# Three of a tile step's four GpSimd powers taken in one instruction over twelve columns

## What is computed

```python
h  = layernorm(x) * (1 + ca) + sa                  # first normalization: mean and variance
# attention part
hn = w1 * (h * rsqrt(mean(h * h) + 1e-6))          # first RMS norm ("RMS1")
r, k, v, g, w = projections of hn mixed with the token before
S  = exp(-exp(w)) * S + k v                         # a scan over 1024 tokens, 16 heads of 8 x 8
o  = groupnorm(r (S + u k v)) * silu(g)
x1 = h + o @ Wo
h2 = w2 * (x1 * rsqrt(mean(x1 * x1) + 1e-6))       # second RMS norm ("RMS2")
y  = x1 + gelu(h2 @ ffn_w1) @ ffn_w2
x2 = x + ga * y
h3 = layernorm(x2) * (1 + cb) + sb                 # second layernorm ("LN2")
# expert part: softmax gate over 8 experts, the best two per token, gated units, weighted sum
out = x2 + gb * experts(h3)
```

## Time and profile before

| what | value |
|---|---|
| runs of the kernel | 724.88, 728.73 and 729.90 us; median 728.73 us |
| the profiled execution | 725.47 us, of which the profile's span is 723.8 us |
| busy share of the span | PE 85%, PEld 65%, DVE 83%, ACT 72%, POOL 74% |
| token stage | up to about 464 us of the span |
| expert stage | from there to 723.8 us |

### The profile page before, as it was taken

The page is one execution under the profiler, slowest core; times in us unless marked ns, Lnnn a source line. Parts: engine busy times, 40 slices in busy tenths (PEclk is TensorE's granted clock), DMA queues, the critical chain, the costliest instruction groups (busy, mean ns, idle before and its releaser), DMA issues. The chain is left out here.

```text
span 723.8 us, 14261 instructions
## 1 busy us (share of the span) xinstructions
PE 617.0 (85%) x3515; PEld 469.7 (65%) x3515; DVE 602.9 (83%) x1384; ACT 523.0 (72%) x1321; POOL 537.9 (74%) x657
## 2 busy tenths in 40 slices
PE   2556889999999999979789687737899999999994
PEld 0433566667777666648557565615688888888883
DVE  6389989999999999997999846665688888888884
ACT  2656668898888977976766676734677888788883
POOL 5467667899999779899869876575766666666666
PEclk8699989999999999998999899857999999999998
DMA  3999888889999898788778799525565444444420
GB/s 109 259 139 133 117 110 133 132 142 160 149 136 159 128 152 112 155 167 157 152 135 147 170 283 286 220 98 166 118 103 87 79 77 78 79 80 80 76 18 1
DMA packets 103300, 95.58 MB, mean 132 GB/s; under 512 B 14523, under 2 KB 82710, under 8 KB 102966
## 3 DMA queue, kind: packets, MB, share of 16 engines
q1 hardware_dynamic: 85846, 79.69, 58.3%
q0 software_dynamic: 16176, 12.75, 10.0%
q10 hardware_dynamic: 1200, 2.23, 0.9%
HBM read 35.47 MB, written 25.61 MB: 84 GB/s over the span
## 5 line engine op out<-in xcount | busy, mean ns | idle before, releaser
L2063 POOL DMA_INDIRECT out<-res,index x91 | 141.3, 1553 | 66.0 <-DVE res L2145 48.1
L843 POOL TENSOR_TENSOR rs_prod<-rT,state_rows 128x512 f32<-128x512 f32 x128 | 139.4, 1097 | 44.7 <-DVE state_rows L1528 43.2
L1281 PEld LDWEIGHTS ps_k<-w,gel 128*128 128x128 f32 x512 | 63.5, 205 | 16.8 <-issue 14.4
L1281 PE MATMUL ps_k<-w,gel 128*128 128x128 f32 x512 | 66.2, 291 | 2.4 <-ACT gel L1098 1.7
L2112 DVE SCALAR_TENSOR_TENSOR half<-ps_b,xg,sig 128x256 f32<-128x256 f32 x91 | 43.6, 480 | 26.0 <-ACT sig L1991 22.8
L1987 ACT ACTIVATE sig<-ps_a 128x256 f32<-128x256 f32 x91 | 35.1, 385 | 41.6 <-issue 20.7
L1246 PE MATMUL ps_f<-hnT_hi,mix_hi 128*128 128x512 f32 x128 | 54.7, 428 | 8.7 <-DVE hnT_lo L1651 7.6
L2105 DVE SCALAR_TENSOR_TENSOR ps_a<-ps_a,xg,sig 128x256 f32<-128x256 f32 x91 | 44.4, 488 | 10.8 <-ACT sig L1987 6.5
L1941 PEld LDWEIGHTS ps_y<-out_w,gT 128*128 128x128 f32 x364 | 47.3, 191 | 8.9 <-ACT gT L2020 5.2
L2013 ACT ACTIVATE ps_b<-bias_rows 128x512 f32 x89 | 53.0, 595 | 0.0
L1247 PE MATMUL ps_f<-hnT_lo,mix_hi 128*128 128x512 f32 x128 | 52.0, 406 | 0.0
(11 more groups left out here) (357 smaller groups left out, 1995.7 us busy)
## 6 DMA issues: line engine op xcount, KB each, us to landing
v_spread<-vT SPq DMA_DIRECT2D x128, 256.0 KB
xg<-sorted_scratch SPq DMA_DIRECT2D x91, 130.0 KB
xin<-in_L_attn_x SPq DMA_DIRECT2D x16, 256.0 KB, 6.3
x<-in_L_attn_x SPq DMA_DIRECT2D x16, 256.0 KB
out<-x SPq DMA_DIRECT2D x16, 256.0 KB
sorted_scratch<-gel SPq DMA_DIRECT2D x4, 910.0 KB, 8.0
tokens_scratch<-h SPq DMA_DIRECT2D x12, 256.0 KB
raw_w<-in_L_ffn_W ACTq DMA_DIRECT2D x2, 1024.0 KB, 8.1
```

Source lines behind the costliest of these rows:

```text
L843: pool.tensor_tensor(rs_prod[:, p, idx % 4], rT[p][:], state[idx][:, p * NT:(p + 1) * NT], ALU.mult).then_inc(s["rs_ready"], 1)
L1281: mm = pe.matmul(ps_k2[:, q * P:(q + 1) * P], gel[c][:, q * P:(q + 1) * P], w2[:, c, :], start=(c == 0), stop=(c == NF - 1))
L2063: pool.indirect_dma_start(out_rows, bass.IndirectOffsetOnAxis(ap=index[k % RESULTS][:, i:i + 1], axis=0), res[k % RESULTS][:, i, :], None, ...
```

## The change

The three roots of RMS1, RMS2 and LN2 are no longer taken one by one. `ve2`, `ve3`, `ve4` become slices of one tile `ve_all` of 12 columns, `rs2`, `rs3`, `rs4` slices of `rs_all`, and `minus_half` has 12 columns. POOL first does the additions of eps of all lanes that the step has, and then one `pow` over the columns of all of them. One semaphore, `roots_ready`, is raised once a step and takes the place of `rms1_rstd`, `rms2_rstd` and `ln2_rstd`; its count for tile `t` is `t` plus the lane's lag. Steps 7 to 16 have all three lanes (12 columns), steps 5, 6 and 17 to 20 have two (8 columns), the others one. LN1's root stays as it is.

```diff
-        minus_half = sb("minus_half", [P, NQ])
+        minus_half = sb("minus_half", [P, 3 * NQ])
...
+        ssq1, ve_all, rs_all = sb("ssq1", [P, NQ]), sb("ve_all", [P, 3 * NQ]), sb("rs_all", [P, 3 * NQ])
+        (ve2, ve3, ve4), (rs2, rs3, rs4) = ([each[:, i * NQ:(i + 1) * NQ] for i in range(3)] for each in (ve_all, rs_all))
+        RMS1, RMS2, LN2 = 1, 5, 7
...
+            def roots(lanes):
+
+                if lanes:
+                    for lane, t, done in lanes:
+                        after(pool, done, t)
+                    span = slice(lanes[0][0] * NQ, (lanes[-1][0] + 1) * NQ)
+                    pool.tensor_tensor(rs_all[:, span], ve_all[:, span], minus_half[:, span], ALU.pow).then_inc(s["roots_ready"], 1)
...
                 for t, p, b in tile(5):
                     after(pool, s["ssq3_ready"], t)
                     pool.tensor_scalar(ve3[:], ssq3[:], 1.0 / D, EPS_RMS, ALU.mult, ALU.add).then_inc(s["rms2_ve"], 1)
-                    after(pool, s["rms2_ve"], t)
-                    pool.tensor_tensor(rs3[:], ve3[:], minus_half[:], ALU.pow).then_inc(s["rms2_rstd"], 1)
                 for t, p, b in tile(1):
                     after(pool, s["ssq1_ready"], t)
                     pool.tensor_scalar(ve2[:], ssq1[:], 1.0 / D, EPS_RMS, ALU.mult, ALU.add).then_inc(s["rms1_ve"], 1)
-                    after(pool, s["rms1_ve"], t)
-                    pool.tensor_tensor(rs2[:], ve2[:], minus_half[:], ALU.pow).then_inc(s["rms1_rstd"], 1)
                 for t, p, b in tile(7):
                     after(pool, s["ln2_mv"], t)
                     after(pool, s["xn4_ready"], t - 1)
                     pool.tensor_scalar(shift4[:], mv4[:, :, 0], -1.0, 0.0, ALU.mult, ALU.add)
                     pool.tensor_scalar(ve4[:], mv4[:, :, 1], 1.0, EPS_LN, ALU.mult, ALU.add).then_inc(s["ln2_ve"], 1)
-                    after(pool, s["ln2_ve"], t)
-                    pool.tensor_tensor(rs4[:], ve4[:], minus_half[:], ALU.pow).then_inc(s["ln2_rstd"], 1)
-                    after(pool, s["ln2_rstd"], t)
+                roots([(lane, t, done) for lane, lag, done in ((0, RMS1, s["rms1_ve"]), (1, RMS2, s["rms2_ve"]), (2, LN2, s["ln2_ve"])) for t, p, b in tile(lag)])
+                for t, p, b in tile(7):
+                    after(pool, s["roots_ready"], t + LN2, 1, 0)
                     mean_shift(shift4, rs4, s["shift2_ready"])
...
             def normalize_second(t, p):
-                after(act, s["ln2_rstd"], t)
+                after(act, s["roots_ready"], t + LN2, 1, 0)
...
                 for t, p, b in tile(4):
-                    after(act, s["rms2_rstd"], t)
+                    after(act, s["roots_ready"], t + RMS2, 1, 0)
                     scale_rows(h2, h_all[:, t], rs3, s["h2_ready"])
...
                 for t, p, b in tile(0):
-                    after(act, s["rms1_rstd"], t)
+                    after(act, s["roots_ready"], t + RMS1, 1, 0)
                     scale_rows(hn, h_all[:, t], rs2, s["hn_ready"])
```

More of the change, by code:

```diff
@@ L443, in attention_block @@
         staged = h_all[:, TILES - 2:].rearrange("p n q d -> p (n q) d")[:, 0:6]
-        ssq1, ve2, rs2 = sb("ssq1", [P, NQ]), sb("ve2", [P, NQ]), sb("rs2", [P, NQ])
+        ssq1, ve_all, rs_all = sb("ssq1", [P, NQ]), sb("ve_all", [P, 3 * NQ]), sb("rs_all", [P, 3 * NQ])
+        (ve2, ve3, ve4), (rs2, rs3, rs4) = ([each[:, i * NQ:(i + 1) * NQ] for i in range(3)] for each in (ve_all, rs_all))
+        RMS1, RMS2, LN2 = 1, 5, 7
         hn = sb("hn", [P, NQ, P])
@@ L458, in attention_block @@
         o_sum = o_gated = sb("o_row", [P, NT])
-        ssq3, ve3, rs3 = sb("ssq3", [P, NQ]), sb("ve3", [P, NQ]), sb("rs3", [P, NQ])
+        ssq3 = sb("ssq3", [P, NQ])
         h2 = sb("h2", [P, NQ, P])
@@ L467, in attention_block @@
         st4, mv4, shift4 = sb("st4", [P, NQ, 6]), sb("mv4", [P, NQ, 2]), sb("shift4", [P, NQ])
-        ve4, rs4 = sb("ve4", [P, NQ]), sb("rs4", [P, NQ])
         h3 = [sb(f"h3{i}", [P, NQ, P]) for i in range(2)]
@@ L485, in attention_block @@
             "mod_ps mod_copied mod_step mod_ready mod_stored first_mods_ps first_mods_ready setup_step weights_step mix_ready "
-            "ln1_stats ln1_mv ln1_ve ln1_rstd xn1_ready h_scaled h_ready ssq1_ready rms1_ve rms1_rstd hn_ready "
+            "ln1_stats ln1_mv ln1_ve ln1_rstd xn1_ready h_scaled h_ready ssq1_ready rms1_ve roots_ready hn_ready "
             "hnT_ps hnT_ready hnlo_ready k_ps v_ps vT_ready "
@@ L490, in attention_block @@
             "o_ready osq_ready var_ps log_ready root_ready rootsq_ready weighed root_better rsg_ps onorm_ready ogated_ready wo_ps x1_ready "
-            "ssq3_ready rms2_ve rms2_rstd h2_ready h2T_ps h2T_ready h2lo_ready ffn2_ps y_ready y_gated x2_ready "
-            "shift1_ready shift2_ready scan_ready rs_ready kv_ready ln2_stats ln2_mv ln2_ve ln2_rstd xn4_ready h3_scaled h3_ready h3T_ps h3T_ready logits_ps logits_ready "
+            "ssq3_ready rms2_ve h2_ready h2T_ps h2T_ready h2lo_ready ffn2_ps y_ready y_gated x2_ready "
+            "shift1_ready shift2_ready scan_ready rs_ready kv_ready ln2_stats ln2_mv ln2_ve xn4_ready h3_scaled h3_ready h3T_ps h3T_ready logits_ps logits_ready "
             "small_ps small_ready expert_in expert_ps expert_hi expert_lo b1_ready b1_stored bias_in route_step tag_step rows_gated batch_staged tags_kept gain_ready exps_ready ranks_ps totals_ps totals_ready unlisted_ready blank_stored bias_rows_in last_staged gates_in gates_spread tags_set out_w_in listed table_step table_ps").split(),
@@ L974, in step @@
                     after(pool, s["ln1_ve"], t)
-                    pool.tensor_tensor(rs1[:], ve1[:], minus_half[:], ALU.pow).then_inc(s["ln1_rstd"], 1)
+                    pool.tensor_tensor(rs1[:], ve1[:], minus_half[:, 0:NQ], ALU.pow).then_inc(s["ln1_rstd"], 1)
                     after(pool, s["ln1_rstd"], t)
```

## The result

| what | before | changed kernel |
|---|---|---|
| median of six runs, taken together | 729.38 us (724.88 to 732.65) | 737.71 us (735.67 to 741.09) |
| ratio, with its 95% interval | 1 | 1.013 (1.010 to 1.016) |
| the profiled execution: span | 723.8 us | 737.7 us |
| end of the token stage in it | 477.40 us | 488.33 us |

The changed kernel is slower: the medians are 8.3 us, or 1.1%, apart, and the ratio is 1.013. The end of the token stage is taken here as the start of the expert stage's first DVE instruction. (The table ahead of the prediction gives about 464 us; that is where the last tiles' work thins out.)

A forecast was written before the change was run, and what follows sets the result against it. DVE was taken to set the pace without a gap in steps 7 to 11. 7.6 + 0.7 + 0.2 + 1.0 - 0.2 + 0.5 + 1.1 = 10.9 us on 725.5 or 728.7 us; 738.0 us said, range 728 to 745.

The forecast's parts named there:

- The chain: From DVE's moments over POOL's pow and ACT's square back to DVE: 5.16 us, 2.53 of them not the pow.
- On POOL: Started at once, POOL's work would save 0.50 us; waiting for the moments, step 10's scan 4 product begins 0.23 us later.
- The pow: The shared pow on POOL: 2.63 us for twelve columns, 1.82 for eight; 0.20 fixed and 0.202 per column.
- The steady steps: Steps 7 to 11: DVE stalls of 1.59, 1.47, 1.54, 1.46 and 1.52 us before L1559, together 7.6 us.
- Steps 12 and 13: Routing work lies between DVE's moments and L1559: 0.7 us lost in step 12, 0 in step 13.
- Steps 14 to 16: Lateness mostly hidden by DVE's idleness in step 15: 0.2 us in step 14, 0 in 15, 1.0 in 16.
- Steps 17 to 20: Eight-column steps: -0.2 us for 17 and 18 together, 0.5 in step 19, 1.1 in step 20.
- rival 2: Pow costs as forecast, but DVE's waits or ACT's room give back half the sum: 731 to 734 us; chance 0.13.
- Steps 5 and 6: Eight columns, no moments needed, and ACT comes later than the root in both: 0 us.
- The sum: Token stage, all steps added: 10.9 us longer, giving 736.4 or 739.6 us by starting time; 738.0 said.
- Rival 1: POOL's pow mostly fixed, twelve columns 1.02 us, deciding at 1.17: no steady step changes, 722 to 725 us; chance 0.17.
- Rival 3: POOL's pow costs three old ones, 3.03 us: 3.4 us more, 740 to 743 us; chance 0.08.

The follow-up runs named there:

- the first pair: Traces of the first measurement, unmodified kernel before and changed kernel: spans 723.8 and 737.7 us, token stage ending at 477.40 and 488.33 us.
- the second pair: Traces of the kernel before and the changed kernel, both run once more on one chip: medians 727.29 and 737.96 us, ratio 1.015.
- the first trace of before: The profiled execution of the unmodified kernel before in the first measurement: span 723.8 us, median of its runs 729.38 us.
- the repeat of the kernel before: The kernel before run once more, nothing changed, for a trace from the same chip as other runs: 727.29 us.
- the repeat of the changed kernel: The changed kernel run once more, nothing altered, on one chip with the kernel before: 737.96 us against 727.29 us, ratio 1.015.
- the first group: The first timing of the kernel before and the changed kernel: medians 729.38 and 737.71 us, ratio 1.013.

## Why the prediction was right, and where its sum was off

**DVE sets the pace and has no gap**: right. The changed kernel has DVE's busy time of before and 6.0 us of gaps, and a step of 23.35 to 23.41 us for 22.15; 23.6 was forecast.

**The chain**: right in place and nearly in size. What isn't the pow takes 2.59 us for 2.53: 0.70 to the pow for 0.64, because `pow` follows the last addition by 0.37 us and not by the 0.28 of the earlier trace rows; then 0.03, 1.82 and 0.04 for 0.05, 1.80 and 0.04. ACT's wait for the root is 1.4 us (6.9 over five steps) for 1.7, by as much as the pow is shorter.

**On POOL**, the product of scan 4 begins 3.21 us after the moments where it was to be 3.50 and before was 3.27: not later at all, since the pow is shorter.

**The pow**: the mis-sized term. Its mean is 2.30 us where 2.63 was forecast. The trace of before had a single width, and I split its 1.01 us into 0.20 fixed and 0.202 a column. Four, eight, twelve and twenty columns take 1.02, 1.67, 2.30 and 3.56 us: 0.159 us a column and 0.38 fixed. That split was the step that failed. The prediction took 0.20 us for all that is fixed, because nothing suggested a second fixed part four times as large; there is one of 0.18 us, about as large as the first. The decision point, 1.17 us, is far from any reading of it.

**The steady steps** 7 to 11: 7.6 us forecast; the stalls sum to 5.8 us, the five steps to 6.2 us in the first pair and 6.1 in the second. The pow accounts for it: five times 0.33 us less is 6.0.

**Steps 12 and 13**: 0.7 forecast, 2.8 measured in the second pair (1.29 and 1.50). Only 0.75 of it is stall (0.37 and 0.38). The rest is longer instructions of the routing work on DVE, which the last section shows and the prediction had at nothing. In step 12 they come and go: the first trace of before has one too, and its pair gives 0.40 us there. In step 13 they don't: that step is 26.13 us long in both traces of before and 27.65 and 27.63 us in both of the changed kernel, so 1.1 us beside its stall of 0.38 us comes with the change in both pairs, and is no scatter.

**Steps 14 to 16**: 1.2 us forecast (0.2, 0 and 1.0), about 0 measured: +1.10, +0.90 and -2.05 in the second pair. The prediction put step 14's lateness down as hidden by DVE's wait before L1559 in step 15, and step 15's by its idleness before L1590 and behind it. The first did not happen, since that wait grew; the idleness behind it took up most of all three steps' lateness. In the repeat of the kernel before, these are DVE's gaps in that place:

```profile
325.61 0.30 DVE L1559 SCALAR_TENSOR_TENSOR ps_k<-ps_k,o_sq 128x128 f32<-128x128 f32 x1 [2.78 <-ACT o_sq L1118]
328.79 0.69 DVE L1590 TENSOR_TENSOR h_all<-ps_k,h_all 128x512 f32<-128x512 f32 x1 [0.84 <-PE ps_k L1281]
330.95 0.69 DVE L1600 TENSOR_TENSOR room<-ps_f,vT 128x512 f32<-128x512 f32 x1 [1.47 <-issue]
```

and in the repeat of the changed kernel:

```profile
339.05 0.30 DVE L1564 SCALAR_TENSOR_TENSOR ps_k<-ps_k,o_sq 128x128 f32<-128x128 f32 x1 [3.78 <-ACT o_sq L1123]
342.32 0.69 DVE L1605 TENSOR_TENSOR room<-ps_f,vT 128x512 f32<-128x512 f32 x1 [0.34 <-PE ps_f L1257]
```

The wait for ACT has grown by 1.0 us and the two behind it have shrunk from 2.31 to 0.34; in the first pair the three were 5.87 us (two of them are in the earlier trace rows) and one of 3.81 was left. The stall of step 16 itself came (0.78 us, 1.0 forecast). In the second pair the stalls and the longer wait are 1.09 + 1.00 + 0.78 = 2.87 us, the shorter waits give back 1.97, and 0.86 more comes from DVE being busy for less in step 16 (25.40 for 26.26 us), which nothing here explains.

**Steps 17 to 20**: 17 and 18 together +0.4 us in the second pair for -0.2. Step 19's stall grew from 3.86 to 4.24 us, 0.38 for 0.5. Ahead of it, DVE waits for a transfer, which is the wait that was to hide step 18's lateness. In the repeat of the kernel before:

```profile
407.82 0.69 DVE L1523 TENSOR_TENSOR kv<-key,v_spread 128x512 f32<-128x512 f32 x1 [2.02 <-DMA v_spread<-vT]
```

and of the changed kernel:

```profile
418.52 0.69 DVE L1528 TENSOR_TENSOR kv<-key,v_spread 128x512 f32<-128x512 f32 x1 [0.96 <-DMA v_spread<-vT]
```

It is 1.06 us shorter, and step 19 as a whole 0.67 us. In the first pair that wait was no shorter (1.69 and 1.88 us), and step 19 is 0.59 us longer. In step 20, ACT scales `h2` after 1.96 us of waiting for the root (first trace), and DVE's wait for `h3`, the 1.1 us of the sum, grew by 1.0 us in the first pair (2.21 to 3.24) and by 0.4 in the second (2.86 to 3.24). From step 19's L1559 to the end of the token stage it is +0.9 us in the first pair and -1.3 in the second. So rival 2, lateness given back, is true of steps 14 to 16 in both pairs and of steps 19 and 20 in the second alone, and not of steps 7 to 13.

**Steps 5 and 6**, forecast 0: the steps are 0.4 to 0.5 us longer together. In step 5, ACT waits 0.62 us for the shared root and DVE stalls 0.30 us where it had no wait; with RMS2's root alone that stall is not there, with RMS1's and RMS2's shared it is. So the sentence that ACT comes later than the root was wrong for step 5. Step 6's stall of 0.43 us is hardly new: it was 0.38 us before.

**The sum**: 10.9 us forecast for the token stage; 10.9 and 9.8 us measured, of which 0.8 and 2.1 us are already there before step 4, ahead of any shared pow, so 10.1 and 7.7. That the number came out so well has luck in it. By the second pair, the steady steps were 1.5 us too dear and steps 14 to 20 another 4.2, and against that stand 0.4 in steps 5 and 6, 2.1 in steps 12 and 13 and the start's 2.1. By the first pair it is 1.4 and 1.0 too dear against 0.5, 1.2 and 0.8. The two pairs differ by 3.2 us in steps 14 to 20, more than that part of the sum (2.6). And 738.0 us was a choice between 736.4 and 739.6 us; the medians differ by 8.3 us in the first group and 10.7 in the second, and the sum was 10.9.

**The rivals.** Rival 1 (pow mostly fixed, 722 to 725 us) fell with the pow's 2.30 us. The Trainium skill's 2.6 cycles per element (GPSIMD Engine Reference, section 3.1), which would have given it, holds for POOL's products here (1.097 us for 512 columns) but not for a pow: 0.159 us a column is some seventy times as much, an estimate with the 1.2 GHz of the same page's section 1. Rival 3 (3.03 us) fell with the same row. Rival 2 holds in part, as said.

## What to carry to other kernels

Before several small operations are merged into one, ask for each result who takes it, and what stands behind that taker in its queue: the merged instruction gives all results at the time of the last, and the earliest needed one pays. Here, over five steps, a saving of 3.9 us on an engine with slack cost 6 us on the engine without any. The remedy can lie at the taker: work that needs nothing from the late result goes ahead of the wait for it. And a price per column can't be read from one width; a second width must be measured, or both ends of the split be kept in the range.

## What the runs showed of the hardware

**A pow on POOL** costs 0.38 us and 0.159 us for each float32 column of a 128-partition tile, by the means at 4, 8, 12 and 20 columns (1.02, 1.67, 2.30 and 3.56 us).

**A DVE instruction and a POOL instruction that meet: one of the two is longer.** DVE's routing instructions, whose operands all lie in SBUF, vary by more than their size. In the first trace of before:

```profile
240.12 1.11 POOL L843 TENSOR_TENSOR rs_prod<-rT,state_rows 128x512 f32<-128x512 f32 x1
240.19 1.18 DVE L96 TENSOR_TENSOR logits<-logits,small 128x128 f32<-128x128 f32 x1
```

In its repeat:

```profile
239.79 1.28 POOL L843 TENSOR_TENSOR rs_prod<-rT,state_rows 128x512 f32<-128x512 f32 x1
239.84 0.28 DVE L96 TENSOR_TENSOR logits<-logits,small 128x128 f32<-128x128 f32 x1
```

The same DVE instruction takes 1.18 us when it starts 0.07 us behind POOL's product, and ends 0.14 us after it; or it takes 0.28 us, and then POOL's product is 0.19 us longer. The repeat of the changed kernel has the long form (1.12 us), and in step 13 two more of 0.78 and 0.98 us that take 0.32 and 0.42 us in the repeat of before. The three add 1.9 us, which with the 0.75 us of stall is nearly all of the 2.8 us of steps 12 and 13. A pow can be the longer one too. In step 13 of the run with RMS1's and RMS2's roots shared, a pow of eight columns that takes 1.65 us elsewhere takes 0.93 us more, beside a routing scan of DVE:

```profile
272.09 2.58 POOL L849 TENSOR_TENSOR rs_all<-ve_all,minus_half 128x8 f32<-128x8 f32 x1
272.11 1.11 DVE L143 TENSOR_TENSOR_SCAN off<-carry_on,tot 128x476 f32<-128x476 f32 x1
```

The Trainium skill (GPSIMD Engine Reference, section 1) says that POOL shares its SBUF interfaces with VectorE and that they contend when a DVE instruction has two SBUF inputs, as these do; the rows shown agree, with up to 0.9 us on either side. DVE's scans over 512 columns that carry a state on (L1528, `state_rows<-decay,state_rows,...`), whose input `decay` lies in PSUM, are the counterpart: from 133 to 300 us of the first trace of before, they take 1.25 to 1.28 us whether products of POOL run beside them for 1.3 us or not at all. None of the experiments was made for this meeting of the two engines, so its cause is inferred. In the three pairs of rows above, POOL's instruction is the longer one where DVE's began 0.02 or 0.05 us behind it, and DVE's where it began 0.07 us behind; so a shift of a few hundredths of a microsecond goes with another outcome. Single steps with routing work can't be compared between two traces below about 1 us, while steps 7 to 11, which have none, agree within 0.02 us.
